# The last edge sum of a four-layer graph network: one block of 128 edges in eight comes by products of one-hot blocks with the node table in SBUF, and GpSimd gathers the other seven

## What is computed

```python
h = h + segment_sum(e, dst)                  # e: edge features through a small network
neigh = jax.ops.segment_sum(h[src], dst, num_segments=N)
z = h + neigh                                # then two products with batch norm and relu
```

## Time and profile before

| What | Value |
|---|---|
| Median of 3 runs | 7438.11 us (7429.24 to 7439.85) |
| Span of the profiled execution | 5778.8 us |
| Median less span | 1659.3 us |
| The last sum's gathers, from the first to the last | 4727.80 to 5711.73 us of the span |
| POOL busy over the span | 69% |
| PE busy over the span | 59% |

### The profile page before, as it was taken

One profiled execution on the slowest core, in us unless ns is written; L12 is line 12 of the kernel. 1 busy time (PEld: TensorE's weight loads), 2 busy tenths in 40 slices (PEclk: granted clock), 3 DMA queues, 4 the chain that ended last, 5 costly groups with the idle time before them and its releaser, 6 DMA issues. The chain is left out here.

```text
span 5778.8 us, 72791 instructions
## 1 busy us (share of the span) xinstructions
PE 3412.2 (59%) x18712; PEld 3084.7 (53%) x18712; DVE 2595.6 (45%) x8699; ACT 1457.5 (25%) x3506; POOL 3969.2 (69%) x4127
## 2 busy tenths in 40 slices
PE   3777777755433334777777776666676653333334
PEld 3676777634333333577777765566565543333333
DVE  4666656662222222433333356777777661111112
ACT  2222222210000000333333335665666410000002
POOL 6777777607777776577777727777777527777774
PEclk6555555576665565877777788999999875555556
DMA  4333333332222211422222226555666412222111
GB/s 126 107 105 109 108 107 107 82 121 87 62 63 64 61 53 49 139 60 60 60 60 60 60 78 168 160 158 158 159 159 159 109 38 53 53 53 53 53 53 41
DMA packets 392271, 522.01 MB, mean 90 GB/s; under 512 B 105994, under 2 KB 275937, under 8 KB 391513
## 3 DMA queue, kind: packets, MB, share of 16 engines
q0 software_dynamic: 131200, 271.80, 18.9%
q1 hardware_dynamic: 258009, 245.43, 14.0%
q10 hardware_dynamic: 2689, 0.36, 0.0%
HBM read 473.25 MB, written 50.76 MB: 91 GB/s over the span
## 5 line engine op out<-in xcount | busy, mean ns | idle before, releaser
L1047 PE MATMUL PS<-arena,att 128*128 x3328 | 735.4, 412 | 1219.5 <-DMA arena<-tab_h,HT 615.8
L1047 PEld LDWEIGHTS PS<-arena,att 128*128 128x128 f32 x3328 | 685.3, 315 | 1271.3 <-issue 1271.2
L1510 POOL DMA_INDIRECT arena<-tab_x,idx_a x880 | 831.4, 945 | 314.1 <-issue 265.5
L993 POOL DMA_INDIRECT arena<-tab_rel,idx_b x782 | 762.3, 975 | 397.3 <-issue 238.0
L679 POOL DMA_INDIRECT arena<-tab,idx_a x832 | 819.1, 984 | 259.4 <-issue 252.0
L993 POOL DMA_INDIRECT arena<-tab_h,HT x782 | 746.9, 955 | 300.5 <-issue 238.0
L491 POOL DMA_INDIRECT arena<-tab_rel,idx_b x782 | 741.0, 948 | 275.0 <-issue 238.0
L1024 DVE TENSOR_SCALAR att<-iota_row,drel 128x128 f32<-128x128 f32 x832 | 182.0, 307 | 814.5 <-PE PS L1047 814.4
L1020 DVE TENSOR_SCALAR att<-iota_row,drel,wgt 128x128 f32<-128x128 f32 x832 | 222.3, 364 | 694.3 <-PE PS L1047 694.2
L583 DVE TENSOR_TENSOR arena<-arena,PS 128x128 f32 x832 | 240.5, 289 | 598.8 <-PE PS L547 524.1
L543 PE MATMUL PS<-arena,att 128*128 x1664 | 368.3, 362 | 228.8 <-DMA arena<-tab_rel,idx_b 206.2
(11 more groups left out here) (374 smaller groups left out, 5252.6 us busy)
## 6 DMA issues: line engine op xcount, KB each, us to landing
arena<-pair_d SPq DMA_DIRECT2D x220, 256.0 KB
arena<-tab_u SPq DMA_DIRECT2D x880, 64.0 KB
arena<-drel_rows SPq DMA_DIRECT2D x104, 512.0 KB
tab_rel<-arena SPq DMA_DIRECT2D x50, 512.0 KB
arena<-tab_rel,idx_b POOLq DMA_INDIRECT x1564, 2.5
arena<-tab_x,idx_a POOLq DMA_INDIRECT x880
arena<-tab,idx_a POOLq DMA_INDIRECT x832
arena<-tab_h,HT POOLq DMA_INDIRECT x782
```

Of the source, the lines that this page charges most:

```text
L993: pool.indirect_dma_start(out=G[:, o:o + D], out_offset=None, in_=table, in_offset=bass.IndirectOffsetOnAxis(ap=src[:, c:c + 1], axis=0)). ...
L1047: ins = nc.tensor.matmul(acc, M[s % RM][:, k * P:(k + 1) * P], G[:, bass.ds(e * (2 * D) + g * D, D)], start=False, stop=True, skip_group_c ...
L1510: pool.indirect_dma_start(out=G[:, o:o + D], out_offset=None, in_=tab_x, in_offset=bass.IndirectOffsetOnAxis(ap=idx_pair[:, 4 * g + u:4 * ...
```

## The change

The last sum gets a function of its own, `stage_last_sum`. `stage_sum` keeps only what the relational sum uses; its code for that stage does the same as before.

- Sixteen steps, 32 blocks, four groups, make a "quad"; there are 24 (`QUADS`), which cover groups 0 to 95. In each of these groups GpSimd gathers blocks 0 to 6 alone.
- Block 7 of the four groups of a quad (512 edges) comes another way. SP loads the 512 source numbers to all partitions (`SRC`, 24 DMAs). For each of the 25 node tiles VectorE compares them with the tile's node numbers (`select`, line 1122: 128x512, into a ring `SEL` of 8), and TensorE multiplies the tile of `H` by this one-hot matrix and accumulates over the 25 tiles in PSUM's eighth bank (`pick`, line 1146). That gives the 512 rows transposed. ScalarE copies them to SBUF (`ROWS_T`), TensorE transposes the four 128x128 pieces back (`turn`, line 1153), and ScalarE copies them to places 7 of the four groups in the ring `G`.
- The picks of a quad stand ahead of the sums of the three first sets of the quad before it: 8, 8 and 9. `turn` stands ahead of the sum of the fourth.
- The wait of `G`'s reuse, the one-hot blocks of the sum and the sum itself stay as they were.

```diff
+        def stage_last_sum(name, table):
+            RG, RM, NS, GROUPS_N, QUADS = 16, 4, 8, -(-ST // 4), ST // 16
...
+            last_src = t["src"][0:16 * QUADS].rearrange("(q u v) e -> q u v e", u=4, v=4)
...
+            def gathers(g):
+                return 7 if g < 4 * QUADS else min(8, 2 * ST - 8 * g)
+            def chunks(s):
+                q, v = s // 4 + 1, s % 4
+                return [(q, c) for c in range(*((0, 8), (8, 16), (16, NT), (0, 0))[v])] if q < QUADS else []
+            with nc.Block() as block:
+                @block.sync
+                def _(sp):
+                    sp.dma_start(src, t["src_t"]).then_inc(s_ix, 16)
+                    for q in range(QUADS):
+                        if q >= 2:
+                            sp.wait_ge(sel_done, NT * (q - 1))
+                        sp.dma_start(SRC[q % 2].rearrange("p (u e) -> p u e", u=4),
+                                     last_src[q, :, 3, P:2 * P].unsqueeze(0).to_broadcast([P, 4, P])
+                                     ).then_inc(s_src[q % 2], 16)
...
+                    for g in range(GROUPS_N):
+                        if g >= RG:
+                            pool.wait_ge(sum_done, g - RG + 7)
+                        for c in range(8 * g, 8 * g + gathers(g)):
...
+                @block.scalar
+                def _(act):
+                    for q in range(QUADS):
+                        act.wait_ge(pick_done, NT * (q + 1))
+                        nc.scalar.copy(ROWS_T, BANK).then_inc(rows_done, 1)
+                        act.wait_ge(turn_done, q + 1)
+                        if 4 * q >= RG:
+                            act.wait_ge(sum_done, 4 * q + 3 - RG + 7)
...
+                    def select(q, c):
+                        i = NT * q + c
...
+                        if i >= NS:
+                            dve.wait_ge(pick_done, i - NS + 1)
+                        dve.tensor_scalar(SEL[i % NS], SRC[q % 2], node[:, c:c + 1], None, ALU.is_equal
+                                          ).then_inc(sel_done, 1)
...
+                    def pick(q, c):
+                        i = NT * q + c
+                        pe.wait_ge(sel_done, i + 1)
+                        if c == 0 and q:
+                            pe.wait_ge(made, q)
+                        nc.tensor.matmul(BANK, H[:, c * D:(c + 1) * D], SEL[i % NS], start=(c == 0),
+                                         stop=(c == NT - 1)).then_inc(pick_done, 1)
...
+                    for s in range(SETS):
+                        for q, c in chunks(s):
+                            pick(q, c)
+                        if s % 4 == 3 and s // 4 + 1 < QUADS:
+                            turn(s // 4 + 1)
...
+                        if s % 4 == 0 and s // 4 < QUADS:
+                            pe.wait_ge(made, s // 4 + 1)
...
-        stage_sum("s5", tab_h, False)
+        stage_last_sum("s5", tab_h)
```

More of the change, by code:

```diff
@@ L960, in stage_sum @@
             M = [att[:, 1024 * i:1024 * (i + 1)] for i in range(RM)]
[L961 removed]
+            src, typ = idx_row, HT[:, 2 * ST:4 * ST].bitcast(I32)
             pos = HT[0:1, 2368:2368 + SS].bitcast(I32)
@@ L1029, in _ @@
                 def _(pe):
-                    parts = aside.tensor(pe) if aside else {}
+                    parts = aside.tensor(pe)
                     pe.wait_ge(s_zero, 1)
```

130 lines of the change are left out of this document (96 added, 34 removed).

## The result

| | Before | Changed |
|---|---|---|
| Median | 7438.11 us (7429.24 to 7442.93, 5 runs) | 7389.71 us (7387.18 to 7406.21, 5 runs) |
| Ratio | | 0.9945, 95% interval 0.9931 to 0.9958 |
| The profiled execution: its own time | not given | 7388.11 us |
| Its span | 5778.8 us | 7386.4 us |
| Last sum, first gather start to last | 983.9 us | 1052.1 us |

What follows compares the result with a forecast made beforehand. It took POOL's issue of gathers, 1.252 us each, to bound the last sum. Gathers removed (-126.1 us) plus contention (+20) made -106, so 7438.1 - 106 = 7332 us, range 7305 to 7425.

Steps and rivals of the forecast that it cites:

- the likeliest case: Whole kernel: 7332 us, between 7312 (no contention) and 7370 (49 us of it and the start's stall); chance 66%.
- I carry that difference over unchanged: Whole kernel: the 1659.3 us between the profiled span and the median of the runs stay the same after the change.
- the late start of the sums: Start of the last sum: first set near 4768 instead of 4745, behind 33 picks; the ring covers it by 41 us.
- the contention: Last sum: DVE's 600 selects lengthen POOL's gathers by 20 us in all, 49 if spread out and each loses 0.12.
- the gathers taken out: Last sum: 686 gathers in place of 782 save 120.2 us, with the first gather's stall 126.1.
- So the stage is as long as its gathers take to issue: Last sum: POOL's gathers set its length, at 1.252 us each, 0.94 of work and 0.30 of issue.
- At full clock PE has 5.8 us to spare in each quad and sets nothing.: Last sum: a quad takes PE 29.3 us at 2.4 GHz, against 35.1 us for POOL's 28 gathers.
- The rival of bursts: Last sum: gathers lose turns to whole bursts of DVE; 7370 to 7423 us, 7384 if half cost 1.09; chance 12%.
- The whole lock: Last sum: each select stops POOL for its whole length, 204 us in all, giving 7516 us, slower; chance 8%.
- PE's clock as the bound: Last sum: PE becomes the bound as its clock falls; half its work at 1.2 GHz gives 7548 us; chance 7%.
- The first gather's stall: Start of the last sum: the first gather's 6.87 us in place of 0.95 is gone, saving 5.9 us.
- The tail: End of the last sum: the seven last sets run as before, 15.24 us, with no picks ahead of them.

Runs made afterwards that it cites:

- 5790 series: Series of timings on one chip in which the unchanged kernel before took 5790 or 5804 us; the shown trace of before, span 5778.8 us, fits these.
- 7450 series: Series of timings on one chip in which the unchanged kernel before took between 7435 and 7456 us; the shown times are among them.
- the picks alone: Changed kernel with only the first eight selects and one load of sources, all picks, turns and copies kept: 7377.39 us, 0.9888 of the kernel before.
- the seven gathers: Changed kernel without the eighth block's loads, selects, picks, turns and copies, so seven gathers of eight remain: 7317.48 us, 0.9815 of the kernel before.
- a ring of two: Changed kernel with two select buffers in place of eight: 5720.64 us (0.9858 of before) in one series, 7410.40 us (0.9935) in another.
- Selects that nothing spaces: Changed kernel with the 600 selects and 24 source loads but no picks, turns or copies: 7431.64 us, 0.9962 of the kernel before.

## Why the prediction was right or wrong

The sign and the range held (7389.71 in 7305 to 7425), the amount did not: 48 us for 106. It lies outside the likeliest case's own 7312 to 7370. The step that failed is "I carry that difference over unchanged": it took a trace of one condition for the times of another. What it hid is the late start of the sums, put at nothing and measured at 33 us. Beside it one term of the sum was mis-sized in both conditions, the contention: 20 forecast, 48.7 measured in the 5790 series and 43 net of waits in the 7450 one. That the range held all the same is partly luck: the gathers taken out gave 11 us more in that condition than I had counted. By its steps:

- **"So the stage is as long as its gathers take to issue", with the pace of 1.252.** True of the shown trace and of the 5790 series. In the 7450 condition the pace was 1.424, with 133 us of ring waits in the stage. 96 gathers fewer gave 137 us of the stage there, not 126.
- **"I carry that difference over unchanged."** This is the step that failed. The 1659.3 us were stalls inside the program, the last sum's 128 among them (1112.1 less 983.9), in executions in which PE, DVE and SyncE start their work late while GpSimd gathers. A difference of 29% between a span and the times of the same kernel was no constant to add at the end; it said that the trace and the times stood for two conditions. In one of them every statement about room was open.
- **"At full clock PE has 5.8 us to spare in each quad and sets nothing."** Right in the 5790 series: no idle time of POOL. Wrong in the 7450 series: POOL does wait for PE, and the picks alone cost 46 us of the stage, 34 at the start and 0.6 a quad afterwards. The granted clock was 0.84 in the stage, just under the 0.85 that I named; what part it has in the waits is not shown.
- **Contention: "I take 20", with 49 as the upper bound.** Mis-sized. It is 48.7 us in the 5790 series, and in the 7450 one the gathers are 67 us longer (excess of the changed kernel less that of the seven gathers). I had argued that a select that comes alone leaves room behind it. It does, for itself; but the estimate by dense passes of line 1224, with gathers 0.06 to 0.12 longer, came from two gathers, and the spread case of 49 was the better reading. With 49 the forecast would have been 77 us of gain, and the 5790 series show 81 and 74. In that condition no other term was clearly off.
- **The rival of bursts.** Its price came nearest (7384 us), its mechanism only in part. The held gathers exist, 13 in the 5790 series and 16 in the shown trace, but beside runs of selects and not of one-hot blocks, and with a ring of two, which forbids them, 7 us were gained.
- **The whole lock.** It was to decide from 0.21 us a select. Selects that nothing spaces cost 0.28, and even so that stage was 13 us shorter than before (1099.0 for 1112.1), because POOL's waits shrank by 61 us. At the picks' pace it is 0.081.
- **PE's clock as the bound.** It did not come in the 5790 series (0.91, no idle time of POOL). In the 7450 series PE does hold POOL up, at a clock of 0.84 and with late starts that the kernel before has too, at 0.57.
- **The first gather's stall, the late start of the sums, the copies.** The first gather takes 0.96 us, as counted. In the 5790 series nothing of the late start reaches POOL, and PE waits 0.8 us in all for ScalarE's second copy. In the 7450 series the 41 us of cover that I had counted for the late start of the sums are gone: POOL's first wait for a set is 20.6 us with seven gathers only, when no pick stands ahead, and 52.7 in the changed kernel. That is 32 us for a step that I put at nothing, the largest single piece of idle time that the change adds.
- **The tail.** 66.1 us from the last gather to the end in the 5790 series, 67.1 before, as forecast. In the 7450 condition it is 83.3 for 80.6, and not the seven last sets alone: seven MATMULs of picks and 14 sets are still to do.

So the 58 us that were missing are accounted for as follows in the 7450 series. The gathers taken out save 137.0 us of the last sum, 11 more than forecast. Against that stand 33.4 for the start (forecast: 0), 43.3 for longer gathers net of waits (forecast: 20) and 0.3 behind the quads; 60.0 remain (1112.1 less 1052.1). The rest, 11.6 us to the measured 48.4, is 2.7 in the tail; 8.9 I have not placed. The two traces come from different series, and stages that the change does not touch differ between them by more than that (1401.7 and 1374.4 us for the first stage's gathers), so the balance closes no further than this. Nor does it say what a cure of one item would give: with 60 us of excess taken away the stage was 6 us shorter.

## What to carry to other kernels

Before a trace is used for a sum, its span must agree with the times that are to be forecast; where they differ by more than a few us, what lies between need not be a constant, and the room of engines that the trace shows may not be there. If an engine's work is replaced by work on its neighbours, price the neighbours' hold on it from a spread-out case, not from two instructions in a dense one. A cost that is measured alone holds only for the spacing that it was measured with: here the two costs, 46 and 124 us, came to 77 together. And where two resources bind in turn, relieving one (60 us of excess) moves its time into the other (66 us of idle), so count the wait before you count the work.

## What the runs showed of the hardware that I had not expected

- One program has two times: 5784 to 5812 us in some series, 7426 to 7476 in others, with three quarters of the difference (1224 of 1683 us) in gather stages. In the longer one TensorE's distances over 0.6 us during the last sum's gathers lie at multiples of 0.7 us (423 of 494), SyncE issues a copy in 5.79 us for 1.71, and 2 to 16 us after the last gather all is dense again. The cause stays open.
- A gather lasts through a run of seven or eight 128x512 selects (2.95 and 3.15 us; the longest was 11.64), while a select alone is stretched by the gather, from 0.49 to 0.69 us. Costs to gathers: 0.28 us a select in runs, 0.08 at the picks' pace.
- The same one-hot block on ScalarE takes two passes of 0.71 us, and the gathers' excess falls by almost three quarters, from 57.0 to 15.6 us, when 16 of 25 are made there.
